# A four-layer graph network: part of the attention logits made by GpSimd instead of VectorE

## The chip, the cores and the metric

The kernel runs on one core of one Trainium2 chip. The metric is the device time of one execution in microseconds, lower is better. The core's engines run side by side and meet at semaphores: PE (TensorE), DVE (VectorE), ACT (ScalarE), POOL (GpSimd), and SP (SyncE), which here only issues DMAs.

## The reference, cut to what matters

The network has four layers on 3125 nodes and 100000 edges: two graph convolutions, a graph attention of 4 heads (the layer of the change), and a transformer-like attention of 4 sublayers. The third layer computes, with self loops added to the edges:

```python
h = (x @ W).reshape(N, H, C)                    # N 3125, H 4, C 32
a_src = jnp.einsum('nhc,hc->nh', h, att_src)
a_dst = jnp.einsum('nhc,hc->nh', h, att_dst)
logits = jax.nn.leaky_relu(a_src[src] + a_dst[dst], 0.2)
m = segment_max(logits, dst)
e = jnp.exp(logits - m[dst])
alpha = e / segment_sum(e, dst)[dst]
out = segment_sum(h[src] * alpha[:, :, None], dst).reshape(N, H * C)
out = elu(batchnorm(out + x @ W_res + bias))
```

## The kernel before, in words

The graph is held densely. A first stage counts the edges of every pair of nodes into two arrays in HBM: `counts_dram`, and `bias_dram`, whose entries are the logarithm of twice the count, or a very negative number where there is no edge. Nodes stand in 25 tiles of 125 (`T`, `NT`), all numbers are float32.

`graph_attention` (line 927) has three stages. In the first, DVE makes two vectors for each head, the "lines": line 0 is a_src (L1016) and line 1 is 0.2 a_src (L1017). They are turned and stored to `lines_dram`, and the per-destination scalar `a_dst` is kept as 0.8 a_dst (L1019). Since leaky_relu(v) = max(v, 0.2 v) for v = a_src + a_dst, the logits less the constant 0.2 a_dst of a row are max(line 0 + 0.8 a_dst, line 1), and a row's constant falls out of the softmax.

The second stage is the loop of the change. A unit is one head of one block of 125 destinations: 100 units (`UNITS`), in two halves. In a half, units alternate between two heads (g = 0 and 1) and go through the 25 blocks. What one unit does, over a row buffer `row` of 125 x 3125, of which there are three (`RING`):

- SP loads the lines of a head, broadcast to 125 partitions, into `line[g]` at the start of each half (`load_lines`, L1064). The reload for the second half waits until the logits of units 48 and 49 are made (L1066). SP also loads the bias of a block for two units (`load_bias`, two buffers, freed by the maximum). It issues the lines' reload after the bias of block 25.
- DVE, `logits` (L1091): one operation makes all 3125 logits from the two lines and the scalar a_dst. It waits for the lines and for the row buffer (L1090), that is for the last transpose of unit n-3.
- DVE, `maximum` (L1100): a custom operation adds the bias in place and takes the maximum of the row; its accumulator is read out, and L1103 makes the negated maximum `neg`, also against the self loop's logit. DVE's order is written out by hand: maximum of n, then logits of n+1.
- ACT (L1122): the exponential in place, with the sum. Then for unit n-1 the copies of the transposed pieces from PSUM (L1135, three of 1000 columns, and L1138, one of 125).
- PE: transposes of 125 x 125 in four pieces of 8, 8, 8 and 1 (`PIECES`, L1182) into three PSUM banks, and two pieces later the products with the values (L1160). A bank is free once ACT has copied it, so the last piece of a unit follows ACT's copy of its first. Each four units, `gather` adds four partial sums (L1171), with two ACT copies around it (L1127, L1145).

POOL has no work in this loop. The third stage normalises and applies batch norm and ELU. `CHUNKS` cuts the 3125 columns into 4 chunks of 500 and 3 of 375, so `CHUNKS[5][0]` is 2375.

The prediction also reads operations outside the loop that use POOL: in the transformer, L1454 (a cast of a 125-column query block), L1457 (a subtraction of such blocks), L1461 (an addition over 125 x 3200), and L1550 (DVE's maximum there, with the scores in PSUM and the bias in SBUF as inputs). L1601 is the affine step after a layer norm: both inputs lie in SBUF, and POOL takes 1152 columns of it (two operations in a row) and DVE 2048 (two as well).

Of the kernel before, what the change touches and what calls it, by code (L numbers as in the profile page):

```python
# [17 lines left out]
ALU = mybir.AluOpType  # L18
# [4 lines left out]
T = 125  # L23
NT = N // T
# [3 lines left out]
CHUNKS = [(T * (3 * c + min(c, FULL)), T * (3 * c + 3 + min(c + 1, FULL))) for c in range(NC)]  # L28
# [34 lines left out]
LANDED = 32  # L63
# [863 lines left out]
def graph_attention(nc, G):  # L927

    HEADS, CH, SLOPE, EPS = 4, 32, 0.2, 1e-5
    LN2 = float(np.log(2.0))  # L930
    PIECES = ((0, 8), (8, 16), (16, 24), (24, 25))
    NP, RING, LAG = len(PIECES), 3, 2
    UNITS, SET = HEADS * NT, 4
    with ExitStack() as ctx:
        sem = lambda name: ctx.enter_context(nc.semaphore(name))
        sbo = lambda name, shape, dt=FP32: ctx.enter_context(nc.sbuf_tensor(name, shape, dt))
# [5 lines left out]
        a_dst = sbo("a_dst", [T, NT, HEADS])  # L942
# [5 lines left out]
        with ExitStack() as pre:  # L948
# [15 lines left out]
            with nc.Block() as block:  # L964
# [43 lines left out]
                @block.vector  # L1008
                def _(dve):
                    m = Marks(pre_dve)  # L1010
                    src, dst = a_own[:, :, 0:HEADS], a_own[:, :, HEADS:]
                    line_of = lambda k: lines[:, k, :, :].rearrange("p h t -> p t h")
                    bank = banks.full(dve, "own", 0)
                    dve.tensor_copy(a_own[:, :, :], bank[0:T, 0:NT * 8].rearrange("p (t k) -> p t k", k=8)).then_inc(banks.read["dve"], 1)
                    banks.done(dve, "own", 1)
                    dve.tensor_copy(line_of(0), src)  # L1016
                    dve.tensor_scalar(line_of(1), src, SLOPE, None, ALU.mult).then_inc(lines_made, 1)  # L1017
                    dve.wait_ge(lines_made, 1)
                    chain(dve, m, dve.tensor_scalar(a_dst[:, :, :], dst, 1.0 - SLOPE, None, ALU.mult))  # L1019
                    chain(dve, m, dve.tensor_tensor(own[:, :, :], src, a_dst[:, :, :], ALU.add))  # L1020
                    chain(dve, m, dve.scalar_tensor_tensor(out=own[:, :, :], in0=src, scalar=SLOPE, in1=own[:, :, :],
                                                           op0=ALU.mult, op1=ALU.max))
                    chain(dve, m, dve.tensor_scalar(own[:, :, :], own[:, :, :], LN2, None, ALU.add))
                    dve.tensor_scalar(neg_own[:, :, :], own[:, :, :], -1.0, None, ALU.mult)
                    for name, out in (("vals", vals.rearrange("p t h w -> p t (h w)")), ("res", res)):
                        for c in range(NC):
                            ts = tiles_of(c)
                            bank = banks.full(dve, name, c)
                            dve.tensor_copy(out[:, ts[0]:ts[-1] + 1, :], rows_view(bank, c, D)).then_inc(banks.read["dve"], 1)

        with ExitStack() as loop:
            sb = lambda name, shape, dt=FP32: loop.enter_context(nc.sbuf_tensor(name, shape, dt))
            line = [sb(f"line{g}", [T, 2, N]) for g in range(2)]
# [9 lines left out]
            line_in = [sem(f"line_in{g}") for g in range(2)]  # L1043
            bias_in = [sem(f"gbias_in{p}") for p in range(2)]
            logits_made = sem("logits_made")
            max_done = sem("gmax_done")
            neg_done = sem("gneg_done")
            exp_done = sem("gexp_done")
# [8 lines left out]
            def unit(n):  # L1057

                half, b, g = n // (2 * NT), n // 2 % NT, n % 2
                return half, b, g, 2 * half + g  # L1060
            with nc.Block() as block:
                @block.sync
                def _(sp):
                    def load_lines(half, g):  # L1064
                        if half:
                            sp.wait_ge(logits_made, 2 * NT * half - 1 + g)  # L1066
                        for j in range(2):
                            one = G["lines_dram"][j, :, :].rearrange("(h t) p -> h (t p)", h=HEADS)[2 * half + g:2 * half + g + 1, :]
                            load_rows(sp, line[g][:, j, :], one.broadcast_to([T, N]), line_in[g])

                    def load_bias(i):
                        if i >= 2:
                            sp.wait_ge(max_done, 2 * (i - 2) + 2)
                        sp.dma_start(bias[i % 2][:, :], G["bias_dram"][i % NT, :, :]).then_inc(bias_in[i % 2], 16)
                    load_lines(0, 0)
                    load_bias(0)
                    load_lines(0, 1)
                    for i in range(1, 2 * NT):
                        load_bias(i)
                        if i == NT:  # L1080
                            for g in range(2):
                                load_lines(1, g)

                @block.vector
                def _(dve):
                    def logits(n):
                        half, b, g, k = unit(n)
                        dve.wait_ge(line_in[g], 2 * LANDED * (half + 1))
                        if n >= RING:
                            dve.wait_ge(turn_ready, NP * (n - RING + 1))  # L1090
                        dve.scalar_tensor_tensor(out=row[n % RING][:, :], in0=line[g][:, 0, :], scalar=a_dst[:, b, k:k + 1],  # L1091
                                                 in1=line[g][:, 1, :], op0=ALU.add, op1=ALU.max).then_inc(logits_made, 1)

                    def maximum(n):
                        half, b, g, k = unit(n)
                        i = n // 2
                        dve.wait_ge(bias_in[i % 2], 16 * (i // 2 + 1))
                        dve.wait_ge(logits_made, n + 1)
                        here = row[n % RING][:, :]
                        dve.tensor_tensor_reduce(out=here, in0=here, in1=bias[i % 2][0:T, :], scale=1.0, scalar=-3.0e38,  # L1100
                                                 op0=ALU.add, op1=ALU.max, accum_out=top[n % 2][:, :]).then_inc(max_done, 1)
                        dve.wait_ge(max_done, n + 1)
                        dve.scalar_tensor_tensor(out=neg[:, b, k:k + 1], in0=top[n % 2][:, :], scalar=-1.0, in1=neg_own[:, b, k:k + 1],  # L1103
                                                 op0=ALU.mult, op1=ALU.min).then_inc(neg_done, 1)
                    m = Marks(pick_made)
                    chain(dve, m, dve.tensor_tensor(pick[:, :], ident[:, 0:CH], ident[:, CH:2 * CH], ALU.add))
                    for j in (2, 3):
                        chain(dve, m, dve.tensor_tensor(pick[:, :], pick[:, :], ident[:, j * CH:(j + 1) * CH], ALU.add))
                    logits(0)
                    for n in range(UNITS):  # L1110
                        maximum(n)
                        if n + 1 < UNITS:
                            logits(n + 1)

                @block.scalar
                def _(act):
# [578 lines left out]
```

## Time and profile before

| | |
|---|---|
| median of three runs | 3591.96 us (3589.69 to 3600.06) |
| the profiled execution's own time | 3577.69 us |
| its span, first to last instruction | 3575.9 us |
| mean granted clock of TensorE | 0.901 |
| attention loop of the third layer | from 1066 to 1823 us |
| DMA | 406.94 MB, 114 GB/s on average |

The profile is of one execution. Its busy shares hold for the whole span and mix many stages, so the stretch of the loop is read by itself. In the views a group of instructions is given by line, engine and operation, then busy time and mean length, then the engine's idle time just before them and what ended most of it. "PEq" or "DVEq" is an engine's sequencer. A tile's name stands without its buffer number: `grow` is the row buffer, `line` the two lines, `gturned` the PSUM banks of transposes, `gwcol` their copies in SBUF.

### The profile page before, as it was taken

To read this page: it belongs to the slowest core of one execution; us is meant where nothing else is said; L and a number is where in the kernel's file an instruction comes from. 1 tells how busy PE (TensorE), PEld (TensorE's weight loads), DVE (VectorE), ACT (ScalarE), POOL (GpSimd) and SP (SyncE) were. 2 spreads that over 40 slices of the span, in tenths; PEclk is the share of its full clock that TensorE was granted. 3 is DMA by queue.
4 is the path that set the end of the run, shared out by engine and by line. 5 is a ranking of instruction groups with operands and counts; after the bars stand their busy time and mean duration, and the time that the engine had idled before them with its cause. 6 is when DMAs were issued, how large, how long until landed. Compare 5 with 4: busy or idle time off the path is not lost. (4 is left out here: it accounts for less than half of the span.)

```text
span 3575.9 us, 62935 instructions
## 1 busy us (share of the span) xinstructions
PE 2732.2 (76%) x21705; PEld 2253.7 (63%) x21705; DVE 2265.9 (63%) x4930; ACT 1603.1 (45%) x2753; POOL 158.2 (4%) x272
## 2 busy tenths in 40 slices
PE   2877786534437888788846999689995999879995
PEld 1555554312235666566635989678994899759985
DVE  8999997100058999799975555545555555545555
ACT  2555554100026888688843444334443444434442
POOL 1000000000000000000000000100010000110011
PEclk9999998766668999899878999899998999989998
DMA  2678777796524333533302333133321333123330
GB/s 55 145 153 155 161 145 168 178 222 156 125 70 129 114 117 115 159 109 109 109 22 75 112 125 110 38 109 125 110 105 35 132 112 121 54 95 112 120 125 20
DMA packets 163526, 406.94 MB, mean 114 GB/s; under 512 B 122245, under 2 KB 134583, under 8 KB 134838
## 3 DMA queue, kind: packets, MB, share of 16 engines
q1 hardware_dynamic: 163363, 404.79, 39.6%
q8 instruction: 99, 1.62, 0.2%
q14 instruction: 64, 0.52, 0.1%
HBM read 322.96 MB, written 80.77 MB: 113 GB/s over the span
## 5 line engine op out<-in xcount | busy, mean ns | idle before, releaser
L1550 DVE CUSTOM_DVE_ANT_0 arow<-scores,abias 125x500 f32<-125x500 f32 (+1 forms) x700 | 434.4, 622 | 516.4 <-issue 425.3
L1486 PE MATMUL asum<-vals,awcol 125*125 125x129 f32 x5000 | 688.4, 277 | 47.0 <-DVE awcol L923 46.5
L1486 PEld LDWEIGHTS asum<-vals,awcol 125*125 125x125 f32 x5000 | 606.3, 187 | 83.2 <-DVE awcol L923 71.6
L1521 ACT ACTIVATE arow<-arow,aneg 125x500 f32<-125x500 f32 (+1 forms) x700 | 431.0, 658 | 129.0 <-DVE aneg L1556 129.0
L921 ACT ACTIVATE awcol<-aturned 125x500 f32<-125x500 f32 (+1 forms) x300 | 163.7, 546 | 693.2 <-PE aturned L1495 693.2
L1182 PE MATMUL gturned<-ident,grow 125*125 125x125 f32 x2500 | 407.3, 304 | 27.2 <-ACT grow L1122 27.2
L1182 PEld LDWEIGHTS gturned<-ident,grow 125*125 125x125 f32 x2500 | 330.1, 203 | 105.4 <-issue 73.4
L1495 PEld LDWEIGHTS aturned<-ident,arow 125*125 125x125 f32 x2500 | 373.7, 187 | 31.3
L1495 PE MATMUL aturned<-ident,arow 125*125 125x125 f32 x2500 | 385.2, 271 | 0.0
L1091 DVE SCALAR_TENSOR_TENSOR grow<-line,a_dst 125x3125 f32<-125x3125 f32 x100 | 347.6, 3476 | 53.6 <-DMA line<-lines_dram 42.7
L1100 DVE CUSTOM_DVE_ANT_0 grow<-grow,bias 125x3125 f32<-125x3125 f32 x100 | 341.7, 3417 | 15.6 <-DVE grow L1091 1.0
L1122 ACT ACTIVATE grow<-grow,neg 125x3125 f32<-125x3125 f32 x100 | 290.3, 2903 | 136.0 <-DVE neg L1103 136.0
L1160 PE MATMUL gparts<-gwcol,h_mem 125*32 125x125 f32 x5000 | 244.8, 290 | 126.4 <-ACT gwcol L1135 126.4
L1477 PE MATMUL scores<-k_low,q_high 128*125 128x500 f32 (+1 forms) x700 | 315.9, 451 | 30.4 <-DVE atop L1550 20.1
L1135 ACT ACTIVATE gwcol<-gturned 125x1000 f32<-125x1000 f32 x300 | 281.1, 1001 | 15.1 <-PE gturned L1182 15.0
L923 DVE COPY awcol<-aturned 125x500 f32<-125x500 f32 (+1 forms) x400 | 244.0, 610 | 26.4 <-PE aturned L1495 26.4
L1477 PE MATMUL scores<-k_high,q_low 128*125 128x500 f32 (+1 forms) x700 | 260.1, 372 | 0.0
L1477 PE MATMUL scores<-k_high,q_high 128*125 128x500 f32 (+1 forms) x700 | 259.0, 370 | 0.0
L1160 PEld LDWEIGHTS gparts<-gwcol,h_mem 125*32 125x32 f32 x5000 | 133.2, 114 | 183.5 <-ACT gwcol L1135 90.8
L405 DVE TENSOR_SCALAR hot_key<-iota_key,fixed 128x325 bf16<-128x325 f16 x1000 | 230.7, 304 | 6.1 <-issue 6.1
L807 PE MATMUL conv_sum<-counts,u_wide 125*32 125x500 f32 (+1 forms) x700 | 97.0, 672 | 171.4 <-DMA counts<-counts_dram 167.3
L517 ACT ACTIVATE blk<-win 125x325 f32<-125x325 f32 x250 | 96.6, 441 | 249.6 <-PE win L473 249.6
(263 smaller groups left out, 3261.7 us busy)
## 6 DMA issues: line engine op xcount, KB each, us to landing
abias<-bias_dram SPq DMA_DIRECT2D x100, 1562.5 KB, 6.5
bias<-bias_dram SPq DMA_DIRECT2D x50, 1562.5 KB, 6.5
counts<-counts_dram SPq DMA_DIRECT2D x41, 1367.2 KB
bias_dram<-lnrow SPq DMA_DIRECT2D x25, 1562.5 KB, 7.8
counts_dram<-blk SPq DMA_DIRECT2D x25, 1367.2 KB
line<-lines_dram SPq DMA_DIRECT2D x8, 1367.2 KB
counts<-counts_dram SPq DMA_DIRECT2D x41, 158.7 KB
fixed<-kp SPq DMA_DIRECT2D x250, 4.0 KB, 2.9
```

What stands on the lines that cost most here:

```text
L923: ins = eng.tensor_copy(out[:, 0:z - a], bank[:, 0:z - a])
L1091: dve.scalar_tensor_tensor(out=row[n % RING][:, :], in0=line[g][:, 0, :], scalar=a_dst[:, b, k:k + 1], in1=line[g][:, 1, :], op0=ALU.add, ...
L1100: dve.tensor_tensor_reduce(out=here, in0=here, in1=bias[i % 2][0:T, :], scale=1.0, scalar=-3.0e38, op0=ALU.add, op1=ALU.max, accum_out=top ...
L1122: act.activation(row[n % RING][:, :], row[n % RING][:, :], ACT.Exp, bias=neg[:, b, k:k + 1], accum_out=den[:, b, k:k + 1]).then_inc(exp_do ...
L1135: act.activation(wcol[q % RING][:, :].rearrange("p (g n) -> p g n", g=2), bank[q % RING][:, :, 0:C4], ACT.Copy).then_inc(col_copied, 1)
L1160: last = pe.matmul(part_ps[CH * j:CH * (j + 1), at:at + T], vals[:, t, k, :], wcol[q % RING][:, (t - t0) * T:(t - t0 + 1) * T], start=(t < ...
L1182: last = pe.transpose(bank[q % RING][:, j // 4, j % 4 * T:(j % 4 + 1) * T], row[n % RING][:, t * T:(t + 1) * T], ident[0:T, 0:T])
L1477: last = pe.matmul(s_ps[c % S_BANKS][:, 0:z - a], left[p][:, :], right[:, a:z], start=(n == 0), stop=(n == len(terms) - 1))
L1486: last = pe.matmul(sum_ps[p][:, :], wcol[c % T_BANKS][:, j * T:(j + 1) * T], vals[:, t, :], start=(t == 0), stop=(t == NT - 1))
L1495: last = pe.transpose(bank[c % T_BANKS][:, j * T:(j + 1) * T], row[p][:, t * T:(t + 1) * T], ident[0:T, 0:T])
L1521: act.activation(row[p][:, a:z], row[p][:, a:z], ACT.Exp, bias=neg[p][:, :]).then_inc(exp_done, 1)
L1550: dve.tensor_tensor_reduce(out=row[p][:, a:z], in0=s_ps[c % S_BANKS][:, 0:z - a], in1=bias[p][0:T, a:z], scale=1.0, scalar=-3.0e38, op0=AL ...
```

## The change

The last 750 of the 3125 sources of every unit (`SPLIT` = 2375 and on) go to POOL, the others stay with DVE. For those columns line 0 is stored as 0.8 a_src, by an additional DVE operation before the loop. POOL then makes the logits in two operations: max(line 0 + 0.8 a_dst, 0), and that plus line 1. This is the same value, 0.2 a_src + max(0.8 (a_src + a_dst), 0). The second waits for the first through the semaphore `shifted`. POOL waits for the lines and the row buffer as DVE does, and for its own earlier unit. `maximum` now also waits for POOL's part, and so does SP before it reloads the lines.

```diff
--- before.py
+++ after.py
@@ -931,6 +931,7 @@
     PIECES = ((0, 8), (8, 16), (16, 24), (24, 25))
     NP, RING, LAG = len(PIECES), 3, 2
     UNITS, SET = HEADS * NT, 4
+    SPLIT = CHUNKS[5][0]
     with ExitStack() as ctx:
         sem = lambda name: ctx.enter_context(nc.semaphore(name))
         sbo = lambda name, shape, dt=FP32: ctx.enter_context(nc.sbuf_tensor(name, shape, dt))
@@ -1013,7 +1014,8 @@
                     bank = banks.full(dve, "own", 0)
                     dve.tensor_copy(a_own[:, :, :], bank[0:T, 0:NT * 8].rearrange("p (t k) -> p t k", k=8)).then_inc(banks.read["dve"], 1)
                     banks.done(dve, "own", 1)
-                    dve.tensor_copy(line_of(0), src)
+                    dve.tensor_copy(line_of(0)[:, 0:SPLIT // T, :], src[:, 0:SPLIT // T, :])
+                    dve.tensor_scalar(line_of(0)[:, SPLIT // T:, :], src[:, SPLIT // T:, :], 1.0 - SLOPE, None, ALU.mult)
                     dve.tensor_scalar(line_of(1), src, SLOPE, None, ALU.mult).then_inc(lines_made, 1)
                     dve.wait_ge(lines_made, 1)
                     chain(dve, m, dve.tensor_scalar(a_dst[:, :, :], dst, 1.0 - SLOPE, None, ALU.mult))
@@ -1043,6 +1045,8 @@
             line_in = [sem(f"line_in{g}") for g in range(2)]
             bias_in = [sem(f"gbias_in{p}") for p in range(2)]
             logits_made = sem("logits_made")
+            logits_made_pool = sem("logits_made_pool")
+            shifted = sem("gshifted")
             max_done = sem("gmax_done")
             neg_done = sem("gneg_done")
             exp_done = sem("gexp_done")
@@ -1064,6 +1068,7 @@
                     def load_lines(half, g):
                         if half:
                             sp.wait_ge(logits_made, 2 * NT * half - 1 + g)
+                            sp.wait_ge(logits_made_pool, 2 * NT * half - 1 + g)
                         for j in range(2):
                             one = G["lines_dram"][j, :, :].rearrange("(h t) p -> h (t p)", h=HEADS)[2 * half + g:2 * half + g + 1, :]
                             load_rows(sp, line[g][:, j, :], one.broadcast_to([T, N]), line_in[g])
@@ -1088,14 +1093,15 @@
                         dve.wait_ge(line_in[g], 2 * LANDED * (half + 1))
                         if n >= RING:
                             dve.wait_ge(turn_ready, NP * (n - RING + 1))
-                        dve.scalar_tensor_tensor(out=row[n % RING][:, :], in0=line[g][:, 0, :], scalar=a_dst[:, b, k:k + 1],
-                                                 in1=line[g][:, 1, :], op0=ALU.add, op1=ALU.max).then_inc(logits_made, 1)
+                        dve.scalar_tensor_tensor(out=row[n % RING][:, 0:SPLIT], in0=line[g][:, 0, 0:SPLIT], scalar=a_dst[:, b, k:k + 1],
+                                                 in1=line[g][:, 1, 0:SPLIT], op0=ALU.add, op1=ALU.max).then_inc(logits_made, 1)
 
                     def maximum(n):
                         half, b, g, k = unit(n)
                         i = n // 2
                         dve.wait_ge(bias_in[i % 2], 16 * (i // 2 + 1))
                         dve.wait_ge(logits_made, n + 1)
+                        dve.wait_ge(logits_made_pool, n + 1)
                         here = row[n % RING][:, :]
                         dve.tensor_tensor_reduce(out=here, in0=here, in1=bias[i % 2][0:T, :], scale=1.0, scalar=-3.0e38,
                                                  op0=ALU.add, op1=ALU.max, accum_out=top[n % 2][:, :]).then_inc(max_done, 1)
@@ -1111,6 +1117,20 @@
                         maximum(n)
                         if n + 1 < UNITS:
                             logits(n + 1)
+
+                @block.gpsimd
+                def _(pool):
+                    for n in range(UNITS):
+                        half, b, g, k = unit(n)
+                        pool.wait_ge(line_in[g], 2 * LANDED * (half + 1))
+                        if n >= RING:
+                            pool.wait_ge(turn_ready, NP * (n - RING + 1))
+                        if n:
+                            pool.wait_ge(logits_made_pool, n)
+                        here = row[n % RING][:, SPLIT:]
+                        pool.tensor_scalar(here, line[g][:, 0, SPLIT:], a_dst[:, b, k:k + 1], 0.0, ALU.add, ALU.max).then_inc(shifted, 1)
+                        pool.wait_ge(shifted, n + 1)
+                        pool.tensor_tensor(here, here, line[g][:, 1, SPLIT:], ALU.add).then_inc(logits_made_pool, 1)
 
                 @block.scalar
                 def _(act):
```

## Rows read from the trace of the kernel before

**Rows 1.** The page, part 1: busy time, share of the span, instructions.

```profile
PE 2732.2 (76%) x21705; PEld 2253.7 (63%) x21705; DVE 2265.9 (63%) x4930; ACT 1603.1 (45%) x2753; POOL 158.2 (4%) x272
```

**Rows 2.** Stretches of the span: stretch, length, busy us (x instructions) by engine, PEclk, DMA share, GB/s.

```profile
1066.00:1823.00 757.00, 619.84 (x7508) 481.88 (x7508) 698.85 (x400) 593.48 (x661) 0.00 (x0) 0.90 0.35 119
```

**Rows 3.** Groups by line in the attention loop, 1066 to 1823 us (idle before, releaser last).

```profile
L1091 DVE SCALAR_TENSOR_TENSOR grow<-line,a_dst 125x3125 f32<-125x3125 f32 x100 | 347.6, 3476 | 53.6 <-DMA line<-lines_dram 42.7 <-PE gturned L1182 10.6 <-issue 0.3
L1100 DVE CUSTOM_DVE_ANT_0 grow<-grow,bias 125x3125 f32<-125x3125 f32 x100 | 341.7, 3417 | 15.6 <-DVE grow L1091 1.0 <-DMA bias<-bias_dram 0.6
...
L1122 ACT ACTIVATE grow<-grow,neg 125x3125 f32<-125x3125 f32 x99 | 287.4, 2903 | 136.0 <-DVE neg L1103 136.0
...
L1103 DVE SCALAR_TENSOR_TENSOR neg<-gtop,neg_own 125x1 f32<-125x1 f32 x100 | 16.0, 160 | 3.5
```

**Rows 4.** Waits in the same stretch: us in total, times, longest.

```profile
ACT grow L1122 <- DVE neg L1103: 136.0, 67, 22.0
...
DVE grow L1091 <- DMA line<-lines_dram: 42.7, 4, 14.8
...
DVE grow L1091 <- PE gturned L1182: 10.6, 9, 2.1
```

**Rows 5.** Timeline of all engines around two units: start, length, instruction, idle before.

```profile
1402.11 3.48 DVE L1091 SCALAR_TENSOR_TENSOR grow<-line,a_dst 125x3125 f32<-125x3125 f32 x1
1402.22 2.90 ACT L1122 ACTIVATE grow<-grow,neg 125x3125 f32<-125x3125 f32 x1 [1.32 <-DVE neg L1103]
...
1405.72 3.42 DVE L1100 CUSTOM_DVE_ANT_0 grow<-grow,bias 125x3125 f32<-125x3125 f32 x1
...
1406.72 0.37 PE L1182 MATMUL gturned<-ident,grow 125*125 125x125 f32 x1
...
1409.18 0.16 DVE L1103 SCALAR_TENSOR_TENSOR neg<-gtop,neg_own 125x1 f32<-125x1 f32 x1
...
1409.26 3.48 DVE L1091 SCALAR_TENSOR_TENSOR grow<-line,a_dst 125x3125 f32<-125x3125 f32 x1
...
1417.59 2.90 ACT L1122 ACTIVATE grow<-grow,neg 125x3125 f32<-125x3125 f32 x1
...
1423.99 0.37 PE L1182 MATMUL gturned<-ident,grow 125*125 125x125 f32 x1
```

**Rows 6.** Timeline of DVE at the change of the lines, halfway through the loop.

```profile
1463.32 3.48 DVE L1091 SCALAR_TENSOR_TENSOR grow<-line,a_dst 125x3125 f32<-125x3125 f32 x1 [8.59 <-DMA line<-lines_dram]
```

**Rows 7.** Timeline of the transformer's affine step, where POOL and DVE run L1601 together.

```profile
2305.26 2.61 POOL L1601 TENSOR_TENSOR h_mem<-h_mem,rows 125x1152 f32<-125x1152 f32 x1 [51.06 <-DVEq L1624]
2305.27 4.75 DVE L1601 TENSOR_TENSOR h_mem<-h_mem,rows 125x2048 f32<-125x2048 f32 x1 [0.18 <-DVE h_mem L125]
...
2307.94 4.53 POOL L1601 TENSOR_TENSOR h_mem<-h_mem,rows 125x1152 f32<-125x1152 f32 x1
2310.05 4.58 DVE L1601 TENSOR_TENSOR h_mem<-h_mem,rows 125x2048 f32<-125x2048 f32 x1
```

**Rows 8.** Groups by line under one long POOL operation (2247 to 2254 us), then before it.

```profile
L1461 POOL TENSOR_TENSOR h_mem<-h_mem,rows 125x3200 f32<-125x3200 f32 x1 | 7.0, 7002 | 0.0
...
L1550 DVE CUSTOM_DVE_ANT_0 arow<-scores,abias 125x500 f32<-125x500 f32 x3 | 2.0, 676 | 1.1 <-issue 1.0
...
L1550 DVE CUSTOM_DVE_ANT_0 arow<-scores,abias 125x500 f32<-125x500 f32 x94 | 63.3, 676 | 46.9 <-issue 24.8 <-PE scores L1477 11.8 <-DMA abias<-bias_dram 8.9
```

**Rows 9.** Groups by line of DVE, whole span: two-input operations with DVE to itself.

```profile
L1236 DVE TENSOR_TENSOR work<-work,total 125x800 f32<-125x800 f32 x4 | 4.0, 992 | 0.1
...
L763 DVE TENSOR_TENSOR work<-h_mem,small 125x3200 f32<-125x3200 f32 x1 | 3.5, 3493 | 0.0
```

**Rows 10.** Groups by line of POOL, whole span.

```profile
L1457 POOL TENSOR_TENSOR q_low<-q,q_high 128x125 fp32r<-128x125 f32 x100 | 43.5, 435 | 18.1 <-POOL q_high L1454 18.1
...
L1454 POOL CAST q_high<-q 128x125 fp32r x96 | 27.9, 291 | 1223.2 <-DVE atop L1550 1102.4 <-DVEq L1539 120.9
...
L535 POOL MEMSET lnrow<- 32x3125 f32 x1 | 2.7, 2699 | 46.0 <-POOLq L175 46.0
```

## The prediction

> **What bounds the kernel now.** I read the page first: over the whole span PE is busy 76%, DVE 63% and POOL 4% [rows 1], an average over stages that says little. The change lies in the attention loop, so the next view is the stretch from 1066 to 1823 us: of its 757 us DVE is busy 699, PE 620, ACT 593 and POOL 0, with a mean granted clock of 0.90 [rows 2]. DVE is busy 92% there. The groups by line say with what: 100 times L1091 (the logits, 3476 ns), L1100 (bias and maximum, 3417 ns) and L1103 (160 ns) [rows 3]. The waits show who waits for whom: ACT's exponential waited 67 times for L1103, while DVE waited for the transposes only 9 times, 10.6 us in all, and four times for the lines' DMA, 42.7 us [rows 4]. The timeline gives the rhythm: L1091 starts at 1402.11 and again at 1409.26, a period of 7.15 us, and ACT sat idle 1.32 us before its exponential [rows 5]. So DVE's serial work sets the pace in about two units of three, and whatever DVE gains or loses per unit counts, a loss in every unit.
>
> A second number is needed for the order of things. The last transpose of unit n-3 frees the row buffer for unit n. It ended at 1407.09, 4.87 us after the exponential of unit n-2 began at 1402.22; with a low clock the same distance was 1424.36 less 1417.59, 6.77 us [rows 5].
>
> **Part 1, the shorter DVE operation.** Two-input DVE operations took 992 ns for 800 elements and 3493 ns for 3200 [rows 9]: 1.042 ns an element and about 0.16 us fixed. L1091 loses 750 elements, so 0.78 us per unit.
>
> **Part 2, two POOL operations per unit.** Two-input POOL operations took 2.61 us for 1152 elements [rows 7] and 7.00 us for 3200 [rows 8]: 2.144 ns an element and 0.14 us fixed. For 750 elements that is a body of 1.61 us, 1.75 with the fixed part. POOL's tensor_scalar is not in the trace. Nearest is the cast with one input, 291 ns for 125 elements [rows 10]: less the same 0.14 it is 1.2 ns an element, 0.90 us for 750. The bounds are the memset, 2699 ns for 3125, so at most 0.65 us for 750 [rows 10], and the two-input body, 1.61 us. I take the cast, since it too reads one tensor and writes one. POOL has nothing else in this loop [rows 2]; some 2.8 us would fit easily into a period of 7, if they ran beside DVE.
>
> **Part 3, whether they run beside DVE.** This decides. In the affine step POOL (1152 elements) and DVE (2048) both run two-input operations from SBUF [rows 7]. By rows 9 a DVE operation of 2048 should take 2.29 us; these took 4.75 and 4.58. The times fit a strict alternation. POOL starts at 2305.26 and ends at 2307.87; DVE ends at 2310.02, 2.15 later, which is its body. The second POOL operation, issued at 2307.94, ends at 2312.47, 2.45 after DVE's end, again its body alone. The second DVE operation ends at 2314.63, 2.16 after that. Nothing overlaps but the fixed 0.14. Against this, the POOL operation of 7.00 us ran over DVE's L1550, of which one input lies in PSUM, and both kept their times: 676 ns under it and 676 before it [rows 8]. So the hindrance comes with two SBUF inputs on DVE. L1091 reads line and line, L1100 reads row and bias, all SBUF, and by their 3476 and 3417 ns each moves an element in the same 1.04 ns: they are of the hindered kind, though no row shows these two operations against POOL. I take it that they alternate with it.
>
> The Trainium skill has a rule for this and it speaks against the change: a DVE instruction with two SBUF inputs contends with a GpSimd instruction that reads SBUF, and whoever starts first keeps the shared port for its whole instruction (SBUF — State Buffer, "Who interferes with whom"). By that rule both new operations come on top of DVE's time; by rows 8 taken alone neither would. The affine step agrees with the rule, with 4.75 us for 2.29.
>
> On the length of the one-input operation the skill differs from my row: bodies of up to two instructions run at 1.03 cycles an element (GPSIMD Engine Reference, "3.1 Elementwise — side-by-side cycle accounting"), at the 1.2 GHz it uses there 0.64 us for 750. By that estimate the sum would be some 25 us smaller. No run here shows a POOL tensor_scalar.
>
> **The new rhythm.** L1100 of unit n now waits for POOL's second operation of n; behind it on DVE stand L1103 and the next L1091, and ACT waits for L1103. In order: L1091; then POOL's second operation, queued since it started (1.61 us of body); then L1100. POOL's first operation of the next unit needs the row buffer, free 4.87 us after the exponential, by then within L1100; so it starts as L1100 ends, and L1103 and the next L1091 wait for its 0.90 us, less the 0.14 us fixed part of DVE that it hides. Per unit: -0.78 + 1.61 + 0.90 - 0.14 = +1.59 us, a period of 8.74.
>
> ACT and PE have room: at 7.15 ACT still idled 1.32 us, and the row buffer of even the low-clock unit (6.77) comes before the 7.9 us at which L1100 would end.
>
> **What hides some of it.** The four line waits stand at units 0, 1, 50 and 51. The work of unit 0, of 49 (after the load for the first half is released) and of 50 lies in front of a DMA wait; the last of these is 8.59 us long [rows 6], so 1.59 more in each is covered. 97 units remain: 97 x 1.59 = 154 us. The 10.6 us of waits for transposes are covered by the longer period: -10.6. SP's added wait puts off the reload of the lines by POOL's second operation, already in unit 48's share; behind it on SP stand bias loads with two buffers, which the line waits cover. The waits on semaphores that are long up cost nothing I can see. One more DVE instruction before the lines are stored costs some 0.2 us. No DMA is added.
>
> **Sum:** 154 - 11 + 0 = +144 us. The profiled execution took 3577.7 us (3575.9 of span and 1.8 around it), so about 3722; the median of the runs is 14.3 us above it, so 3736.
>
> **Rivals.**
> *Faster: no contention in this loop.* Place: L1091 and L1100 under POOL's operations. If their second reads don't meet POOL, they keep 2695 and 3417 ns, and DVE's period falls to 6.4. The gain reaches the end where ACT waited for DVE, 67 units: 67 x 0.78 = 52 us, so 3540. For it: L1550 under POOL [rows 8]. Against it: rows 7. The point from which it decides: POOL's work must lengthen DVE's by less than 0.78 us a unit. Chance 0.05.
> *Same: only L1091 contends.* The custom L1100 would let POOL run under it. POOL's first operation then starts when the row is free, 5.1 us after the last L1103 but one, and ends at 6.1; the second ends at 7.95; L1091 follows (10.5), then L1100 (14.0): two units in 14.1 us, 7.05 each, against 7.15 now. That gives about 3585. For it: L1100 is a custom operation like L1550. Against: it has a second SBUF input. Chance 0.05, of which some lies just outside 0.3%.
> *Slower still: POOL comes too late.* PE, busy 82% now, would be busy less; if the granted clock falls and the row is free only after 7.9 us, POOL's first operation falls behind L1091 and the second follows it at once: 0.38 us more (0.28 of fixed parts, 0.1 for the semaphore) on 97 units, 37 us, 3773. Chance 0.10.
> *Not what it says:* 2375 is where the sixth chunk begins, so sizes are as named; nothing to weigh.
>
> **Numbers.** Forecast 3736 with 0.80. Its own ends: with the memset's rate 0.25 us less a unit, 3712, and 3698 if the second operation hides a fixed part too; with 1.61 for the first operation +0.71 a unit, 3805. The range is 3692 to 3805. A measurement here tells 0.3%, about 11 us, from no change. Faster 0.06, same 0.03, slower 0.91.
>
> **What would show it.** Right: L1091 and L1100 together above 6.12 us a unit by 1.4 or more, or DVE idle before L1100 for POOL; POOL's second operation lasting over 1.75 us where it queued; ACT's wait for L1103 some 150 us longer; a period near 8.7. Wrong: L1091 at 2.70 and L1100 at 3.42 us while POOL runs, or a POOL tensor_scalar far from 1.04 us.

## The result and the profile after

The changed kernel took 3704.89 us (median of 4 runs, 3691.3 to 3706.1), the kernel before 3590.82 in the same comparison. The ratio is 1.0306 with a 95% interval of 1.0274 to 1.0337: slower by 3.1%, about 114 us. The forecast was 3736, slower, with a range of 3692 to 3805. The profiled executions took 3691.30 us (after) and 3577.69 (before), each 13 to 14 us below its median, so their difference, 113.6 us, can stand for that of the medians.

The page, part 1, of the changed kernel, which answers to [rows 1]:

```profile
PE 2784.8 (75%) x21705; PEld 2288.9 (62%) x21705; DVE 2238.0 (61%) x4931; ACT 1604.5 (43%) x2753; POOL 832.5 (23%) x472
```

POOL is busy 674 us more and that did not shorten the kernel: DVE is busy 28 us less and the span is 113.4 us longer. The stretches of the span, with the columns of [rows 2], give the place:

```profile
0.00:1062.00 1062.00, 635.92 (x3543) 415.71 (x3543) 642.32 (x2014) 336.76 (x881) 28.52 (x48) 0.84 0.62 142
1062.00:1938.00 876.00, 670.46 (x7531) 518.40 (x7532) 671.40 (x400) 596.26 (x663) 674.67 (x200) 0.84 0.31 105
1938.00:3690.00 1752.00, 1478.45 (x10634) 1354.82 (x10632) 924.25 (x2517) 671.51 (x1210) 129.35 (x224) 0.94 0.26 94
```

The attention loop, about 757 us before, now takes about 870. What lies before and behind it kept its length within 3 us. DVE is busy 77% of the loop (92% before), and the granted clock fell from 0.90 to 0.84. The groups by line in the loop, with the columns of [rows 3] (L1096 is the old L1091, L1106 the old L1100, L1109 the old L1103, L1142 the old L1122):

```profile
L1131 POOL TENSOR_SCALAR grow<-line,a_dst 125x750 f32<-125x750 f32 x100 | 479.2, 4792 | 231.2 <-PE gturned L1202 151.8 <-DMA line<-lines_dram 79.1 <-POOL grow L1133 0.4
...
L1106 DVE CUSTOM_DVE_ANT_0 grow<-grow,bias 125x3125 f32<-125x3125 f32 x100 | 341.7, 3417 | 174.5 <-POOL grow L1133 174.5
L1142 ACT ACTIVATE grow<-grow,neg 125x3125 f32<-125x3125 f32 x100 | 290.3, 2903 | 242.0 <-DVE neg L1109 241.8
...
L1096 DVE SCALAR_TENSOR_TENSOR grow<-line,a_dst 125x2375 f32<-125x2375 f32 x100 | 269.4, 2694 | 34.9 <-DMA line<-lines_dram 33.8 <-PE gturned L1202 1.1
...
L1133 POOL TENSOR_TENSOR grow<-grow,line 125x750 f32<-125x750 f32 x100 | 195.4, 1954 | 8.3
...
L1109 DVE SCALAR_TENSOR_TENSOR neg<-gtop,neg_own 125x1 f32<-125x1 f32 x100 | 66.9, 669 | 3.5
```

These rows hold the whole account, because DVE is the engine that sets the pace. Against [rows 3], L1096 lost 78.2 us. The idle time before the maximum rose from 15.6 to 174.5, +158.9. The small L1109, which works on one element a partition but also reads two tensors, `gtop` and `neg_own`, rose from 16.0 to 66.9, +50.9. The idle time before L1096 fell from 53.6 to 34.9, -18.7. The sum is +112.9, and the span grew by 113.4. PE with its lower clock has no term in this sum: DVE waited for transposes before L1096 only 1.1 us in all. Whether the clock bears on the late row buffers shown next, no run separates.

The timelines of DVE and POOL show how. First a unit like most (85 of the 99 periods are 8.32 or 8.33 us, where 7.15 stood before), then unit 48, one of seven of another kind:

```profile
1444.68 5.15 POOL L1131 TENSOR_SCALAR grow<-line,a_dst 125x750 f32<-125x750 f32 x1 [1.09 <-PE gturned L1202]
...
1447.21 0.72 DVE L1109 SCALAR_TENSOR_TENSOR neg<-gtop,neg_own 125x1 f32<-125x1 f32 x1
1447.86 2.68 DVE L1096 SCALAR_TENSOR_TENSOR grow<-line,a_dst 125x2375 f32<-125x2375 f32 x1
...
1449.92 1.99 POOL L1133 TENSOR_TENSOR grow<-grow,line 125x750 f32<-125x750 f32 x1
...
1452.08 3.42 DVE L1106 CUSTOM_DVE_ANT_0 grow<-grow,bias 125x3125 f32<-125x3125 f32 x1 [1.54 <-POOL grow L1133]
...
1481.15 2.69 DVE L1096 SCALAR_TENSOR_TENSOR grow<-line,a_dst 125x2375 f32<-125x2375 f32 x1 [0.48 <-PE gturned L1202]
1481.21 5.30 POOL L1131 TENSOR_SCALAR grow<-line,a_dst 125x750 f32<-125x750 f32 x1 [4.33 <-PE gturned L1202]
...
1486.59 1.51 POOL L1133 TENSOR_TENSOR grow<-grow,line 125x750 f32<-125x750 f32 x1
...
1488.27 3.42 DVE L1106 CUSTOM_DVE_ANT_0 grow<-grow,bias 125x3125 f32<-125x3125 f32 x1 [4.43 <-POOL grow L1133]
```

In the first, POOL's first operation is issued at 1444.68 while the maximum of the unit before runs (to 1447.18). L1109 then lasts 0.72 us instead of 0.16. L1096 runs its undisturbed 2.68 us, though POOL's operation goes on beside it until 1449.83. POOL's addition is issued before L1096 ends at 1450.54 and itself ends at 1451.91, 1.37 us after that. In unit 48 the row buffer came late: L1096 started first, POOL's operation ended 2.67 us after L1096 did, the addition took 1.51 alone, and the maximum waited 4.43 us instead of 1.54.

### The profile page after: what moved, and what is told of

It reads as the page before. It is cut to its first block and busy times, and to the rows that moved or that the text cites. A ratio compares the mean times of both kernels' runs of the same rounds, so it can differ in the third digit from the quotient of the medians.

```text
span 3689.3 us, 63237 instructions
## 1 busy us (share of the span) xinstructions
PE 2784.8 (75%) x21705; PEld 2288.9 (62%) x21705; DVE 2238.0 (61%) x4931; ACT 1604.5 (43%) x2753; POOL 832.5 (23%) x472
## 5 line engine op out<-in xcount | busy, mean ns | idle before, releaser
L1131 POOL TENSOR_SCALAR grow<-line,a_dst 125x750 f32<-125x750 f32 x100 | 479.2, 4792 | 231.2 <-PE gturned L1202 151.8
L1202 PE MATMUL gturned<-ident,grow 125*125 125x125 f32 x2500 | 434.3, 318 | 28.3 <-ACT grow L1142 28.3
L1106 DVE CUSTOM_DVE_ANT_0 grow<-grow,bias 125x3125 f32<-125x3125 f32 x100 | 341.7, 3417 | 174.5 <-POOL grow L1133 174.5
L1202 PEld LDWEIGHTS gturned<-ident,grow 125*125 125x125 f32 x2500 | 353.3, 215 | 115.1 <-issue 78.0
L1180 PE MATMUL gparts<-gwcol,h_mem 125*32 125x125 f32 x5000 | 265.9, 312 | 187.7 <-ACT gwcol L1155 187.7
L1142 ACT ACTIVATE grow<-grow,neg 125x3125 f32<-125x3125 f32 x100 | 290.3, 2903 | 242.0 <-DVE neg L1109 241.8
L1474 POOL CAST q_high<-q 128x125 fp32r (+1 forms) x100 | 28.9, 289 | 1272.8 <-DVE atop L1570 1152.0
L1180 PEld LDWEIGHTS gparts<-gwcol,h_mem 125*32 125x32 f32 x5000 | 144.0, 121 | 249.5 <-ACT gwcol L1155 149.6
L1096 DVE SCALAR_TENSOR_TENSOR grow<-line,a_dst 125x2375 f32<-125x2375 f32 x100 | 269.4, 2694 | 34.9 <-DMA line<-lines_dram 33.8
```

Source lines behind the costliest of these rows:

```text
L1096: dve.scalar_tensor_tensor(out=row[n % RING][:, 0:SPLIT], in0=line[g][:, 0, 0:SPLIT], scalar=a_dst[:, b, k:k + 1], in1=line[g][:, 1, 0:SPL ...
L1131: pool.tensor_scalar(here, line[g][:, 0, SPLIT:], a_dst[:, b, k:k + 1], 0.0, ALU.add, ALU.max).then_inc(shifted, 1)
L1142: act.activation(row[n % RING][:, :], row[n % RING][:, :], ACT.Exp, bias=neg[:, b, k:k + 1], accum_out=den[:, b, k:k + 1]).then_inc(exp_do ...
L1180: last = pe.matmul(part_ps[CH * j:CH * (j + 1), at:at + T], vals[:, t, k, :], wcol[q % RING][:, (t - t0) * T:(t - t0 + 1) * T], start=(t < ...
L1202: last = pe.transpose(bank[q % RING][:, j // 4, j % 4 * T:(j % 4 + 1) * T], row[n % RING][:, t * T:(t + 1) * T], ident[0:T, 0:T])
```

## The experiments

Each ratio is to the kernel before, run on the same chip.

**e1, the same POOL work without anybody waiting for it.** DVE makes all 3125 logits, POOL writes to a tile of its own.

```diff
-                        here = row[n % RING][:, SPLIT:]
+                        here = junk[:, :]
...
-                        dve.wait_ge(logits_made_pool, n + 1)
```

> DVE makes all 3125 logits as before; POOL runs the change's two operations on a tile of its own that nobody reads and no engine but SP's line reload waits for, so the wait of L1106 for POOL is gone and only a meeting at SBUF is left. Theory (POOL's reads and DVE's two-input operations exclude each other): the small operation after the maximum grows from 0.16 to about 0.72 us, and the custom maximum lasts 1.1 to 1.3 us longer than 3.42; period near 8.9 us instead of 7.15; 97 units x 1.75 less 11 = +159, about 3750 us. Rival (the time after the change comes only from waiting for a slow POOL): all DVE operations keep their times, 3591 us.

Measured: 3757.04 us, ratio 1.0462 (1.0436 to 1.0488). Groups by line of e1 in the loop:

```profile
L1105 DVE CUSTOM_DVE_ANT_0 grow<-grow,bias 125x3125 f32<-125x3125 f32 x100 | 387.5, 3875 | 15.1 <-DVE grow L1096 1.2
L1096 DVE SCALAR_TENSOR_TENSOR grow<-line,a_dst 125x3125 f32<-125x3125 f32 x100 | 346.9, 3469 | 36.7 <-DMA line<-lines_dram 36.7
...
L1108 DVE SCALAR_TENSOR_TENSOR neg<-gtop,neg_own 125x1 f32<-125x1 f32 x100 | 159.1, 1591 | 3.5
```

No DVE operation waits on POOL by a semaphore, and yet the maximum lasts 3875 ns instead of 3417 and L1108 1591 instead of 160. So POOL's operations stretch DVE's. The price came in other places than expected, since POOL, bound to nobody, fell into another order: 0.46 us on the maximum and 1.43 on the small operation. The period is 9.05 us, 1.9 over that before. The rival, that all of the price is a wait for a slow POOL, is out.

**e2, POOL only writes.** As e1, with memsets in place of both operations.

```diff
-                        pool.tensor_scalar(here, line[g][:, 0, SPLIT:], a_dst[:, b, k:k + 1], 0.0, ALU.add, ALU.max).then_inc(shifted, 1)
+                        pool.memset(here, 0.0).then_inc(shifted, 1)
...
-                        pool.tensor_tensor(here, here, line[g][:, 1, SPLIT:], ALU.add).then_inc(logits_made_pool, 1)
+                        pool.memset(here, 0.5).then_inc(logits_made_pool, 1)
```

> As e1, but POOL's two operations on its own tile are memsets of 750 columns, which write SBUF and read nothing. Theory (only POOL's reads meet DVE's second input): DVE keeps 3.48, 3.42 and 0.16 us, time 3591 within 0.3%. Rival (any POOL operation on SBUF blocks DVE): some 0.5 us per memset, 1.0 a unit, near 3680 us.

Measured: 3584.97 us, ratio 0.9984 (0.9970 to 0.9998), no difference over the 0.3% that can be told. Groups by line of e2:

```profile
L1096 DVE SCALAR_TENSOR_TENSOR grow<-line,a_dst 125x3125 f32<-125x3125 f32 x99 | 344.0, 3475 | 57.5 <-DMA line<-lines_dram 38.4 <-PE gturned L1201 18.8 <-issue 0.3
L1105 DVE CUSTOM_DVE_ANT_0 grow<-grow,bias 125x3125 f32<-125x3125 f32 x98 | 334.8, 3416 | 15.3 <-DVE grow L1096 1.0 <-DMA bias<-bias_dram 0.6
...
L1108 DVE SCALAR_TENSOR_TENSOR neg<-gtop,neg_own 125x1 f32<-125x1 f32 x98 | 15.6, 159 | 3.4
```

All three keep their times beside 200 POOL memsets of 0.72 us each. Writing alone doesn't hold DVE up; the meeting needs POOL's reads.

**e3, the change with memsets instead of the work.** The same edit in the changed kernel: the logits of the last 750 columns are left out, all waits stay.

> The change with POOL's two operations replaced by memsets of the same 750 columns, all waits kept: the logits of those columns are left out (a constant stands there). Theory (reads meet): L1096 2.69 and the maximum 3.42 us with 0.13 us between them, DVE's serial work 6.4 us a unit; faster than before by the cut where ACT waited for DVE, 20 to 52 us, 3540 to 3570. It is what the cut alone would be worth. Rival (the added wait or any POOL write costs by itself): 3591 or more.

Measured: 3497.42 us, ratio 0.9753 (0.9719 to 0.9786), 93 us faster, nearly twice what was expected. Its wait of ACT, and the group of the maximum:

```profile
ACT grow L1142 <- DVE neg L1109: 72.4, 53, 22.0
```

```profile
L1106 DVE CUSTOM_DVE_ANT_0 grow<-grow,bias 125x3125 f32<-125x3125 f32 x100 | 341.6, 3416 | 14.3 <-DMA bias<-bias_dram 1.4
```

The added semaphores cost nothing (14.3 us idle before the maximum, 15.6 before). The shorter DVE operation is worth its full 0.8 us in nearly every unit: 91 of 99 periods are 6.35 or 6.36 us. ACT still waited 53 times. The cut itself is 78 of the 90 us between the two profiles' spans; the idle time before L1096 fell by 7 more. So the change's loss, from 3497 to 3705, comes with what POOL's real operations do and the memsets don't. They read, and they last longer (2.82 and 1.51 us alone, a memset 0.72). In a unit like most the length alone would not make DVE wait: begun at 1444.68, the two would end near 1449.1 if DVE didn't delay them, and L1096 ends at 1450.54. There the price is the meeting. In the late units the length counts too.

**e4, single operations, alone and together.** A stage behind the kernel before; only durations count.

> The kernel before with a stage behind it that runs single operations of POOL and DVE, alone and started together by semaphores; the time is longer by that stage (some 150 us) and says nothing, the durations count. Theory: POOL's tensor_scalar on 750 columns takes 2.7 to 2.8 us alone (in the changed kernel it ended 2.66 us after DVE's maximum) but holds DVE up by only about 0.65 us; its two-input addition with plain operands takes 1.5 us for 750 and holds DVE up by its whole body; with an operand that is broadcast over blocks of 125 it takes 1.75, which is what the row of before showed. Memsets hold nobody up. Rival: tensor_scalar alone takes about 1 us and the rest of its 2.7 us is waiting for DVE.

Timeline of e4: the first three alone, the next two pairs started together, the last a memset under a maximum:

```profile
3591.32 2.82 POOL L1668 TENSOR_SCALAR m_pout<-m_pone,m_sca 125x750 f32<-125x750 f32 x1
...
3601.31 10.37 POOL L1668 TENSOR_SCALAR m_pout<-m_pone,m_sca 125x3000 f32<-125x3000 f32 x1
...
3611.76 1.76 POOL L1673 TENSOR_TENSOR m_pout<-m_pone,m_ptwo 125x750 f32<-125x750 f32 x1
...
3639.60 3.48 DVE L1691 SCALAR_TENSOR_TENSOR m_out<-m_one,m_sca,m_two 125x3125 f32<-125x3125 f32 x1
3639.66 6.08 POOL L1668 TENSOR_SCALAR m_pout<-m_pone,m_sca 125x750 f32<-125x750 f32 x1 [7.26 <-DVE m_top L1693]
...
3693.15 9.81 DVE L1691 SCALAR_TENSOR_TENSOR m_out<-m_one,m_sca,m_two 125x3125 f32<-125x3125 f32 x1 [1.66 <-POOL m_pout L1673]
...
3716.50 2.60 POOL L1675 MEMSET m_pout<- 125x3000 f32 x1 [0.97 <-DVE m_out L1691]
3716.52 3.42 DVE L1693 CUSTOM_DVE_ANT_0 m_out<-m_one,m_bia 125x3125 f32<-125x3125 f32 x1
```

POOL's tensor_scalar takes 2.82 us alone for 750 columns and 10.37 for 3000, about 3.35 ns a column: the theory's number, not the rival's 1 us. One of the two goes through and the other waits: in the first pair DVE kept 3.48 us and POOL stretched to 6.08; in the second an addition of 3000 columns (6.50 us) stretched DVE's 3.48 to 9.81, though DVE's operation began 0.04 us before it. A memset stretched nothing. One guess was wrong: the additions took 1.76 us with plain operands and 1.68 with a broadcast one, so the broadcast is not why they take 1.51 in the loop.

**e5, half the columns.** `SPLIT = CHUNKS[6][0]`, 2750.

> SPLIT at 2750: POOL has 375 columns instead of 750. Theory (POOL's reads hold DVE up by a time in proportion to the columns: 0.56 and 1.40 us at 750): 0.28 + 0.70 - 0.39 = +0.59 a unit, period 7.75; 97 x 0.59 - 11 = +46, near 3637 us. Rival (a fixed price per POOL operation, 1.96 us for two): period 8.7, near 3733 us.

Measured: 3639.1 us, ratio 1.0148 (1.0109 to 1.0187), period 7.74; the theory said 3637 and 7.75. The kernel before took 3587.19 in that comparison, so the difference is 52 us where +46 was expected. Up to 750 columns the price goes by the column, not by the operation (e9 shows where this ends). DVE's cut fell with it: 0.39 us gained and 0.98 paid a unit, so a smaller share for POOL doesn't turn the loss into a gain.

**e6, the first operation alone.** The addition is taken out, so line 1 is not added in the last 750 columns.

```diff
-                        pool.tensor_scalar(here, line[g][:, 0, SPLIT:], a_dst[:, b, k:k + 1], 0.0, ALU.add, ALU.max).then_inc(shifted, 1)
-                        pool.wait_ge(shifted, n + 1)
-                        pool.tensor_tensor(here, here, line[g][:, 1, SPLIT:], ALU.add).then_inc(logits_made_pool, 1)
+                        pool.tensor_scalar(here, line[g][:, 0, SPLIT:], a_dst[:, b, k:k + 1], 0.0, ALU.add, ALU.max).then_inc(logits_made_pool, 1)
```

> The change without POOL's second operation (line 1 is not added in the last 750 columns, that part of the logits is left out). Theory: the first operation holds DVE up by its reads alone, 0.56 us after the maximum, and its remaining 2.1 us run beside L1096, so the maximum waits for nothing; period 6.36 (e3) + 0.56 = 6.92; 3497 + 97 x 0.56 + a few units in which it comes late, near 3560, faster than before. Rival (an exclusive turn for POOL's whole operation, 2.66 us): period 9.0, 3497 + 97 x 2.66 = 3755.

**e7, the addition alone.** POOL adds the two lines into the row; the scalar and the maximum are left out there.

> The change with POOL's addition alone, of the two lines into the row (scalar and maximum are left out in the last 750 columns). Theory: it is ready before the maximum of the unit before ends and runs right behind it; the small operation L1109 waits for its whole body, 1.4 to 1.6 us; period 6.36 + 1.4 to 1.6 = 7.8 to 8.0; 3497 + 97 x 1.5 = 3640, range 3630 to 3655. Together e6 and e7 should make up the change: 54 + 145 over e3, 3497 + 199 = 3696. Rival (the second operation costs only as a wait behind the first): near e3.

e6 measured 3576.03 us, ratio 0.9959 (0.9936 to 0.9982), period 6.91. e7 measured 3622.24, ratio 1.0099 (1.0059 to 1.0138), period 7.53. The group of L1109 first in e6, then in e7:

```profile
L1109 DVE SCALAR_TENSOR_TENSOR neg<-gtop,neg_own 125x1 f32<-125x1 f32 x100 | 62.9, 629 | 3.5
```

```profile
L1109 DVE SCALAR_TENSOR_TENSOR neg<-gtop,neg_own 125x1 f32<-125x1 f32 x100 | 116.9, 1169 | 3.5
```

Over e3's 6.36 us the first operation costs 0.55 a unit, the addition 1.17, though alone they last 2.82 and 1.51. The period of e6 is as expected; its time is 16 us over, because POOL came late in 14 units, not in a few, and each of those waited some 2.6 us more. e7 is 18 us under: the addition behind the maximum held DVE up 1.17 us, less than the 1.4 expected. Both rivals are out. The kernel of e6 is 0.4% faster than the kernel before, but it leaves out one of POOL's two operations, so its logits are not the layer's. The two prices add up to 1.72 us, and the change's 8.32 less 6.36 is 1.96; the other 0.24 appears only when both operations stand in one unit. Its cause is open.

**e9, how long POOL's reads last.** DVE starts 750 columns, POOL's operation stands behind it, more DVE operations (0.99 us each) behind that.

> The kernel before with a stage of single operations behind it. In the first six POOL is alone: a copy, the addition in place and not in place, a tensor_scalar of 125 columns. In the others DVE starts a two-input operation of 750 columns, POOL's operation stands behind it, and three more of DVE behind that; the second of DVE is lengthened by as long as POOL's reads last. Theory: tensor_scalar holds DVE up by 0.86 ns a column up to about 700 columns and by 3.35 ns a column beyond (in e4 it held 3000 columns' reads for 7.8 of 10.2 us), so 0.3, 0.6, 1.7, 2.9 and 5.4 us for 375, 750, 1125, 1500 and 2250; the additions hold it up by their whole body, and in place the addition takes 1.5 us for 750 instead of 1.76. Rival: it is held up by a fixed share of POOL's operation (a quarter at 750).

Timeline of e9: a copy and a tensor_scalar of POOL alone, then each POOL operation with the DVE operation that it held up:

```profile
3597.92 0.81 POOL L1668 COPY m_pout<-m_pone 125x750 f32<-125x750 f32 x1
...
3608.69 0.74 POOL L1663 TENSOR_SCALAR m_pout<-m_pone,m_sca 125x125 f32<-125x125 f32 x1
...
3609.52 2.36 POOL L1663 TENSOR_SCALAR m_pout<-m_pone,m_sca 125x375 f32<-125x375 f32 x1
3610.38 1.31 DVE L1688 SCALAR_TENSOR_TENSOR m_again<-m_one,m_sca,m_two 125x750 f32<-125x750 f32 x1
...
3613.68 3.56 POOL L1663 TENSOR_SCALAR m_pout<-m_pone,m_sca 125x750 f32<-125x750 f32 x1 [1.79 <-DVE m_out L1690]
3614.57 1.54 DVE L1688 SCALAR_TENSOR_TENSOR m_again<-m_one,m_sca,m_two 125x750 f32<-125x750 f32 x1
...
3618.10 4.91 POOL L1663 TENSOR_SCALAR m_pout<-m_pone,m_sca 125x1125 f32<-125x1125 f32 x1 [0.86 <-DVE m_out L1690]
3618.95 4.55 DVE L1688 SCALAR_TENSOR_TENSOR m_again<-m_one,m_sca,m_two 125x750 f32<-125x750 f32 x1
...
3625.49 6.14 POOL L1663 TENSOR_SCALAR m_pout<-m_pone,m_sca 125x1500 f32<-125x1500 f32 x1 [2.48 <-DVE m_out L1690]
3626.34 4.85 DVE L1688 SCALAR_TENSOR_TENSOR m_again<-m_one,m_sca,m_two 125x750 f32<-125x750 f32 x1
...
3633.18 8.68 POOL L1663 TENSOR_SCALAR m_pout<-m_pone,m_sca 125x2250 f32<-125x2250 f32 x1 [1.56 <-DVE m_out L1690]
3634.04 8.07 DVE L1688 SCALAR_TENSOR_TENSOR m_again<-m_one,m_sca,m_two 125x750 f32<-125x750 f32 x1
```

Less its 0.99 us, DVE was held up 0.32, 0.55, 3.56, 3.86 and 7.08 us. Up to 750 columns the expectation holds; beyond, it is wrong: there is a jump between 750 and 1125, and little between 1125 and 1500. An estimate that fits is that POOL reads in pieces of about a thousand columns (0.85 ns a column, from 0.32 us for 375), works each through at 3.35 ns a column, and lets DVE in only once the last piece is read: 0.6 us for 750, 3.35 + 0.1 = 3.5 for 1125, 3.8 for 1500 and 6.7 + 0.2 = 6.9 for 2250. It fits all five sizes, but was made after them; that POOL works in such pieces is not shown. The addition in place took 1.76 us like the other.

**e10, the addition's 1.51 us.** Eleven operations of POOL alone, with other starts of the columns.

> Where POOL's addition of 750 columns gets its 1.51 us in the loop (e7, and the changed kernel where DVE does not hold it up) against 1.76 in e4 and e9. All operations run alone. Theory: the start of the columns decides, since in the loop they begin at column 2375 of 3125: the tail operations take 1.5 us, the plain ones 1.76. Rival: it is something of the loop and not of the operands (what else runs, or the tiles' places), and all here take 1.76.

Both theories fell. Timeline of e10: all operands from column 2375; only the second input shifted by one column; both inputs shifted by one:

```profile
3596.14 1.76 POOL L1669 TENSOR_TENSOR m_pout<-m_pone,m_ptwo 125x750 f32<-125x750 f32 x1
...
3605.38 1.51 POOL L1669 TENSOR_TENSOR m_pout<-m_pone,m_ptwo 125x750 f32<-125x750 f32 x1
...
3606.97 1.76 POOL L1669 TENSOR_TENSOR m_pout<-m_pone,m_ptwo 125x750 f32<-125x750 f32 x1
```

It was faster in the cases in which one input starts at an odd column and the other at an even one. That is so in the loop too: the row starts at 2375 of its tile, line 1 at 3125 + 2375 = 5500 of its own. Why it is faster stays open.

**e8, L1103 given to ACT, nothing on POOL.** Since DVE's serial time is the pace, L1103 is made by ACT in two small operations, and DVE goes from the maximum straight to the next logits.

```diff
-                        dve.wait_ge(max_done, n + 1)
-                        dve.scalar_tensor_tensor(out=neg[:, b, k:k + 1], in0=top[n % 2][:, :], scalar=-1.0, in1=neg_own[:, b, k:k + 1],
-                                                 op0=ALU.mult, op1=ALU.min).then_inc(neg_done, 1)
...
-                            act.wait_ge(neg_done, n + 1)
+                            act.wait_ge(max_done, n + 1)
+                            act.activation(over[:, :], top[n % 2][:, :], ACT.Relu, bias=neg_own[:, b, k:k + 1]).then_inc(over_done, 1)
+                            act.wait_ge(over_done, n + 1)
+                            act.activation(neg[:, b, k:k + 1], over[:, :], ACT.Identity, bias=neg_own[:, b, k:k + 1], scale=-1.0).then_inc(neg_done, 1)
+                            act.wait_ge(neg_done, n + 1)
```

> A version from the kernel before, with nothing on POOL: L1103 goes from DVE to ACT as two operations on 125 x 1 (a Relu and an Identity with scale -1), since DVE's serial time is what counts: e3 gained 93 us for 0.80 us less of it a unit. DVE's period falls from 7.16 by 0.1 to 0.2 us, ACT gets 0.4 to 0.5 us more and still idles. 99 x 0.15 = -15, near 3576. Rival: the longer way from the maximum to the exponential and ACT's added time show at the ends of sets and where ACT sets the pace: 3591 or slower.

Measured over 12 runs: 3575.77 us, ratio 0.9957 (0.9940 to 0.9975), 0.4% faster than the kernel before and some 3.5% faster than the changed one. The expectation, near 3576, holds. Timeline of e8, DVE and ACT:

```profile
1111.34 3.47 DVE L1093 SCALAR_TENSOR_TENSOR grow<-line,a_dst 125x3125 f32<-125x3125 f32 x1
1111.46 0.29 ACT L1123 ACTIVATE gover<-gtop,neg_own 125x1 f32<-125x1 f32 x1 [0.46 <-DVE gtop L1104]
1111.79 0.29 ACT L1125 ACTIVATE neg<-gover,neg_own 125x1 f32<-125x1 f32 x1
...
1118.29 3.47 DVE L1093 SCALAR_TENSOR_TENSOR grow<-line,a_dst 125x3125 f32<-125x3125 f32 x1
```

The period of undisturbed units is 6.94, 0.21 less. Some of the 21 us came back as waits for the row buffer: 23.0 us in this profile, 10.6 in [rows 4].

## Why the prediction was right, and its sizes off

**DVE sets the pace.** Right, and more fully than written: of the 99 periods before, 84 are 7.15 or 7.16 us, which is more than two of three, and in e3 the 0.78 us less a unit came back whole, 93 us in all with shorter waits. The rival *faster* was priced at 52 us by counting only units in which ACT waited. That was the wrong count; by e3 its price would be near 3497, not 3540. The units where ACT didn't wait were not set by ACT, as three row buffers let DVE use its time in the next unit.

**Part 1, the cut.** Right: 0.78 us, 2694 ns.

**Part 3, that POOL and DVE exclude each other with two SBUF inputs on DVE.** Right, for both operations no row had shown: e1 stretches the custom maximum (3417 to 3875 ns), e4 L1091's kind (3.48 to 9.81 us). So the rivals *faster*, without contention, and *same*, in which the maximum lets POOL run, are both out. The rule of the Trainium skill (SBUF — State Buffer, "Who interferes with whom") holds here, down to memsets not meeting DVE (e2). In one point the measurement is finer: the page has whoever issues first keep the shared ports for its whole instruction, and the tensor_scalar of 750 columns held DVE up 0.55 us of its 2.82 (e9).

**The first operation.** Its step took the cast's 1.2 ns a column for both its length and its price, 0.90 us less 0.14. The length was wrong by a factor of 2.7 (2.82 us against 1.04), the price smaller than said, 0.56 us for 0.76. The prediction had named "a POOL tensor_scalar far from 1.04 us" as a sign of being wrong, and that sign came. The forecast stood all the same because length and price are different things here: the operation lasts 2.82 us and holds DVE up 0.55 of them (e9), and its rest runs beside L1096. That a price taken from the cast came near is luck: it was the length of an operation that turned out 2.7 times as long. The Trainium skill's 1.03 cycles an element (GPSIMD Engine Reference, "3.1 Elementwise — side-by-side cycle accounting") gives an estimate of 0.86 ns a column, far from the operation's 3.35.

**The second operation.** The step said a body of 1.61; the maximum waited 1.54 instead of 0.13, about 1.4. The rate of 2.144 ns came from additions whose inputs start alike; here they start at odd and even columns (e10), and 1.51 less 0.14 is 1.37.

**The rhythm.** As written: POOL's first operation right behind the maximum, its second behind L1096. The sum per unit is -0.78 + 1.41 + 0.56 = +1.19 instead of +1.59; the periods say 8.32 - 7.15 = 1.17. That both sizes were set too high, by 0.40 us a unit together, is 39 us over 97 units, more than the miss of 31 us (3736 against 3705). The late units, which the forecast left out, gave 20 us back. Most of the rest is that nine units did not hold L1109 up (5 us) and that more idle time was covered (18.7 us for 15.4). The number came closer than its two sizes by luck.

**POOL too late.** The rival for slower still happened in part, in seven units (1, 48, 50, 51, 56, 72 and 84), four for want of a row buffer and three behind the line waits, where DVE and POOL start together. The four are 48, 56, 72 and 84, each the first of a set of four units, and `gather` runs once a set; no run tests whether that is the cause. It was priced at 0.38 us a unit and cost 4.43 - 1.54 = 2.89, since the slow first operation then lies open: 7 x 2.89 = 20 us. With the exact idle time of 0.16 us before the maximum in [rows 3], the account is: the cut -78, the second operation 93 x 1.38 + 7 x 4.27 = +158, the first 91 x 0.56 = +51, and the idle time before L1096 -19, together +112 of the 113 us of the span. The last term had been forecast as 10.6 and three covered units, 15.4 in all.

**The signs and the range.** Three of the signs for right came: DVE idle before the maximum for POOL (174.5 us), POOL's addition at 1.99 us where it queued, and a longer period, 8.32 for 8.7. ACT's wait for `neg` grew by 106 us, not 150. The lower end of the range, 3692, has no term of its own; the smallest sum worked out was 3698, and 3705 lies close above it.

## What to carry to other kernels

Before work goes from VectorE to an idle GpSimd, look at VectorE's inputs: where its operations read two tensors from SBUF, GpSimd's reads came on top of its time here, 1.96 us a unit for a cut of 0.78, and the idle engine wasn't free. Look for one place in the trace where both already run together, and compare with the length each has alone. Where one engine's serial time set the pace behind three buffers, what was cut from it counted in nearly every unit, also in those where the follower seemed busy (e3).

## What the runs showed of the hardware that was not expected

- GpSimd's tensor_scalar (add, max, float32) took 0.74 us for 125 columns, 2.82 for 750 and 10.37 for 3000, while its copy took 0.81 for 750: so moving the columns is not what takes the time.
- It held a two-input VectorE operation up 0.55 us at 750 columns and 3.56 at 1125.
- GpSimd's addition took 1.51 us instead of 1.76 for 750 columns when its inputs started at columns of unlike parity.
